# First pair's query parts in another order, and twelve units' transposes copied by ScalarE, in a fused attention and feed-forward kernel

## The reference

```python
c_q = hidden_states @ w_q_down                       # 512 -> 192
q_nope = (c_q @ w_q_up_nope) ...                     # 32 heads of 128
q_rope = _apply_rope(c_q @ w_q_up_rope ...)          # 32 heads of 64, rotary
c_kv = hidden_states @ w_kv_down                     # 512 -> 64
k_rope = _apply_rope(hidden_states @ w_k_rope)
q_lat = einsum('bhsd,hdr->bhsr', q_nope, wuk)
scores = (q_lat . c_kv + q_rope . k_rope) / sqrt(192)
probs = softmax(where(causal, scores, min))
out_lat = einsum('bhst,btr->bhsr', probs, c_kv)
out = einsum('bhsr,hdr->bhsd', out_lat, wuv) @ w_out
```

## Time and profile before

| | |
|---|---|
| median of three timed runs | 1170.35 us |
| the profiled execution's own time | 1167.57 us |
| its span, first to last instruction | 1165.8 us |
| mean granted clock of TensorE | 0.992 of full speed |
| TensorE busy with matmuls | 1105.7 us, 95% |
| VectorE, GpSimd, ScalarE busy | 908.2, 740.0, 623.9 us |
| period from batch to batch | 272.9 us |

### The profile page before, as it was taken

One profiled execution on the slowest core, in us unless ns is written; L12 is line 12 of the kernel. 1 busy time (PEld: TensorE's weight loads), 2 busy tenths in 40 slices (PEclk: granted clock), 3 DMA queues, 4 the chain that ended last, 5 costly groups with the idle time before them and its releaser, 6 DMA issues.

```text
span 1165.8 us, 21866 instructions
## 1 busy us (share of the span) xinstructions
PE 1105.7 (95%) x7284; PEld 906.6 (78%) x7284; DVE 908.2 (78%) x2667; ACT 623.9 (54%) x1733; POOL 740.0 (63%) x951
## 2 busy tenths in 40 slices
PE   5896999999998999999999899999999899999997
PEld 4755788888797788888788678888888678888876
DVE  4767888888676888878776888788867787888855
ACT  3554655555454655555535555655545466555542
POOL 2406977887432978787631887787723598877841
PEclk9998999999999999999999999999999999999998
DMA  9660000000101000000101000000010100000000
GB/s 286 179 194 1 1 1 1 1 1 1 37 10 64 2 1 2 1 1 1 37 1 37 37 2 1 2 1 2 1 37 28 47 1 1 1 1 2 1 1 37
DMA packets 22248, 30.96 MB, mean 27 GB/s; under 512 B 9302, under 2 KB 11094, under 8 KB 21498
## 3 DMA queue, kind: packets, MB, share of 16 engines
q1 hardware_dynamic: 19770, 24.85, 6.7%
q10 hardware_dynamic: 2368, 4.72, 1.2%
HBM read 22.23 MB, written 4.19 MB: 23 GB/s over the span
## 4 chain that ended last, share of the span: by engine, by line
PE 79%; DVE 7%; POOL 7%; ACT 3%; issue 2%; SPq 1%; DMA 1%; POOLq 0%; DVEq 0%
PE Y L983 15%; PE Y L957 12%; PE XZ L942 11%; PE Y L906 10%; PE XZ L922 6%; PE XZ L923 6%; PE XZ L921 5%; PE Y L675 4%; POOL prob L631 3%; PE XZ L675 2%; POOL qT_lo L542 2%; PE XZ L650 2%; POOL q_sums L537 2%; DVE xT_lo L1281 1%; ACT xT_hi L1037 1%
## 5 line engine op out<-in xcount | busy, mean ns | idle before, releaser
L1228 ACT ACTIVATE prob<-XZ,small 128x512 f32<-128x512 f32 (+3 forms) x512 | 266.3, 525 | 282.8 <-DVE small L1622 282.8
L631 POOL TENSOR_TENSOR prob<-prob,small 128x512 f32<-128x512 f32 (+3 forms) x512 | 360.7, 721 | 50.1 <-DVE small L1576 40.4
L1622 DVE CUSTOM_DVE_ANT_0 XZ<-XZ,mask 128x512 f32<-128x512 f32 (+3 forms) x512 | 247.9, 506 | 114.6 <-PE XZ L923 110.5
L537 POOL TENSOR_TENSOR q_sums<-q_sums,q_turned 64x512 f32<-64x512 f32 (+2 forms) x130 | 164.2, 1263 | 201.5 <-DVE q_turned L1564 200.1
L942 PE MATMUL XZ<-ident,prob 128*128 128x128 f32 x1280 | 196.3, 276 | 3.2 <-POOL prob L631 2.9
L921 PE MATMUL XZ<-kT_hi,qT_hi 128*128 128x512 f32 (+3 forms) x512 | 176.9, 345 | 12.7 <-ACT prob L1228 6.8
L542 POOL TENSOR_TENSOR qT_lo<-q_sums,qT_hi 128x512 fp32r<-128x512 f32 (+2 forms) x130 | 165.2, 1271 | 31.9 <-ACT qT_hi L1195 31.8
L942 PEld LDWEIGHTS XZ<-ident,prob 128*128 128x128 f32 x1280 | 149.5, 140 | 43.2 <-POOL prob L631 10.6
L922 PE MATMUL XZ<-kT_lo,qT_hi 128*128 128x512 f32 (+3 forms) x512 | 165.4, 323 | 0.0
L923 PE MATMUL XZ<-kT_hi,qT_lo 128*128 128x512 f32 (+3 forms) x512 | 165.2, 323 | 0.0
L957 PE MATMUL Y<-probT,ckv 128*64 128x384 f32 (+2 forms) x1280 | 152.3, 384 | 0.0
(11 more groups left out here) (220 smaller groups left out, 2162.0 us busy)
## 6 DMA issues: line engine op xcount, KB each, us to landing
wout_nat<-in_L_attn_w_out_dram SPq DMA_DIRECT2D x16, 512.0 KB, 5.0
out_dram<-x_sb SPq DMA_DIRECT2D x16, 256.0 KB, 2.0
x_next<-_attn_hidden_states_dram SPq DMA_DIRECT2D x12, 256.0 KB, 3.4
x_sb<-x_next SPq DMA_DIRECT2D x12, 256.0 KB, 2.3
wbase_nat<-in_L_ffn_W_base_dram ACTq DMA_DIRECT2D x1, 1024.0 KB, 5.7
x_sb<-_attn_hidden_states_dram ACTq DMA_DIRECT2D x4, 256.0 KB, 7.0
nope_a<-_L_attn_w_q_up_nope_dram ACTq DMA_DIRECT2D x1, 1024.0 KB, 5.4
rope_a<-_L_attn_w_q_up_rope_dram SPq DMA_DIRECT2D x1, 1024.0 KB, 8.0
```

Source lines behind the costliest of these rows:

```text
L537: nc.gpsimd.tensor_tensor(q, q, turned, ALU.add).then_inc(q_sum_set, 1)
L631: last = nc.gpsimd.tensor_tensor(prob[u % RING][:, c:c + w], prob[u % RING][:, c:c + w], inv_sum[:, u % RING, m:m + 1].broadcast_to([P, w] ...
L1228: last = nc.scalar.activation(prob[u % RING][:, c:c + w], score_ps[u % 2][:, c:c + w], ACT.Exp, bias=neg_max[:, u % RING, m:m + 1], scale= ...
L1622: last = nc.vector.tensor_tensor_reduce(bank, bank, mask[:, S - w:S], -1.0, HIGHEST, ALU.add, ALU.min, neg_max[:, u % RING, m:m + 1])
```

## The change

Five things change. The opening's parts are taken in the order head 0 early, head 0 late, head 1 late, head 1 early; `ckT_low` of the last tile goes ahead of head 1's early rotary, and the late products write a bank of their own, `XZ[1]`. In batches 1 to 3, head 1 is likewise split into a late and an early part for VectorE, GpSimd and ScalarE (its products stay whole); `update_rows` of the last tile moves into slot 1 of the next attention, behind that unit's maximum and the reciprocal of unit 0. In pair 0, the next pair's first queries are issued in slot 1 and not 0, and GpSimd and ScalarE do their part of the next queries after the scaling and the exponential of the slot. Units 0 to 11 of each batch are all copied by ScalarE. The waits of TensorE follow the parts (`first_parts_done`), and `pv` of pair 0 waits for `x_updated`. The diff, cut to its core:

```diff
-ACT_COPIES = (1, 1, 2, 2, 3)
-DVE_COPIES = (0, 1, 1, 2, 2)
+ACT_FIRST = 12
+BY_ACT = tuple(w < ACT_FIRST or w % UNITS in ACT_BANKS for w in range(UNITS * PAIRS))
...
-        FIRST_PARTS = ((0, EARLY), (1, EARLY), (0, LATE), (1, LATE))
+        FIRST_PARTS = ((0, EARLY), (0, LATE), (1, LATE), (1, EARLY))
+        NEXT_PARTS = ((0, ALL), (1, LATE), (1, EARLY))
...
+        def first_parts_done(b, u):
+            return ({0: 2, 1: 3, 3: 4} if b == 0 else {0: next_part(b, 0) + 1, 1: next_part(b, 1) + 1,
+                                                        3: next_part(b, 2) + 1}).get(u)
...
@@ GpSimd @@
+                def queries_by_parts(m, parts):
+                    for j, (head, cols) in enumerate(parts):
                         if j:
-                            before, where = FIRST_PARTS[j - 1]
-                            qT_low(j - 1, before, 0, where)
-                            pool.wait_ge(qT_lo_set, j)
-                        q_sum(j, head, 0, cols)
-                    qT_low(3, 1, 0, LATE)
+                            pool.wait_ge(qT_lo_set, m + j)
+                        q_sum(m + j, head, 0, cols)
+                        qT_low(m + j, head, 0, cols)
...
+                def query_work(b, g, u, scaled):
+                    k, p = u % UNITS, u // UNITS
+                    m = q_index(b, BODY_PAIRS * g + p + 1, k // 2)
+                    if k % 2:
+                        qT_low(m, k // 2, (p + 1) % 2)
+                    else:
+                        pool.wait_ge(prob_scaled, scaled)
+                        q_sum(m, k // 2, (p + 1) % 2)
...
+                        queries = k < 4 and within(g, u, UNITS * LAST_PAIR - 1)
+                        if queries and known(g, u, UNITS):
+                            query_work(b, g, u, 80 * b + BODY * g + u)
                         if within(g, u, SLOTS - 1):
...
                             last.then_inc(prob_scaled, 1)
+                        if queries and not known(g, u, UNITS):
+                            query_work(b, g, u, 80 * b + BODY * g + u + 1)
...
@@ TensorE, opening @@
-                    for j, (head, cols) in enumerate(FIRST_PARTS):
-                        if j == 2:
-                            transpose_down(-1, STEPS - 1)
-                            pe.wait_ge(ckT_hi, ST)
-                            pe.wait_ge(ckT_lo, ST)
-                        if j >= 2:
-                            pe.wait_ge(q_rot_set, j - 1)
-                        q_products(j, 0, head, qT_ps[head], cols)
+                    for head in range(2):
+                        q_products(0, head, qT_ps[head], EARLY)
+                    transpose_down(-1, STEPS - 1)
+                    pe.wait_ge(ckT_hi, ST)
+                    pe.wait_ge(ckT_lo, ST)
+                    for head in range(2):
+                        q_products(0, head, XZ[1][:, head, :], LATE)
...
@@ TensorE, pv @@
+                    else:
+                        pe.wait_ge(x_updated, 8 * b + 4)
...
@@ TensorE, slots @@
-                        if k in (0, 2) and queries:
-                            m = q_index(b, n, k // 2)
-                            if not known(g, u, 1):
-                                pe.wait_ge(x_updated, 8 * b + 4)
-                            pe.wait_ge(q_rot_set, m - 1)
-                            q_products(m, n, k // 2, qT_ps[k // 2])
+                        if queries and k == (0 if known(g, u, UNITS) else 1):
+                            if not known(g, u, UNITS):
+                                pe.wait_ge(x_updated, 8 * b + 3 if b else ST)
+                            pe.wait_ge(q_rot_set, q_index(b, n, 0) - 1)
+                            q_products(n, 0, qT_ps[0])
+                        if queries and k == 2:
+                            pe.wait_ge(q_rot_set, q_index(b, n, 1) - 1)
+                            q_products(n, 1, qT_ps[1])
...
@@ ScalarE, mixed_steps @@
-                    qT_high(q_index(b + 1, 0, 0), 0, 0)
-                    z_high(b, ORDER[-1])
-                    qT_high(q_index(b + 1, 0, 1), 1, 0)
+                    for j, (head, cols) in enumerate(NEXT_PARTS):
+                        if j == 1:
+                            z_high(b, ORDER[-1])
+                        qT_high(next_part(b + 1, j), head, 0, cols)
...
@@ ScalarE, slots @@
-                        if k in (2, 4) and queries:
+                        rounding = k in (2, 4) and queries
+                        if rounding and known(g, u, UNITS):
                             qT_high(q_index(b, n1, k // 2 - 1), k // 2 - 1, (p + 1) % 2)
...
+                        if rounding and not known(g, u, UNITS):
+                            qT_high(q_index(b, n1, k // 2 - 1), k // 2 - 1, (p + 1) % 2)
                         if copies and k != 2:
                             copy_probT(act, nc.scalar, b, g, v)
...
@@ VectorE, opening @@
-                    for j, (head, cols) in enumerate(FIRST_PARTS):
-                        if j == 2:
-                            ckT_low(-1, STEPS - 1)
-                        q_rotary(j, head, 0, qT_ps[head], cols)
+                    q_rotary(1, 0, 0, qT_ps[0], EARLY)
+                    ckT_low(-1, STEPS - 1)
+                    for head in range(2):
+                        q_rotary(3 + head, head, 0, XZ[1][:, head, :], LATE)
+                    q_rotary(2, 1, 0, qT_ps[1], EARLY)
...
@@ VectorE, mixed_steps @@
-                    q_scaled(q_index(b + 1, 0, 1), 1, 0, XZ[1][:, 1, :])
+                    q_rotary(q_count(b + 1, 0, 1) + 1, 1, 0, XZ[1][:, 1, :], LATE)
+                    update_rows(b, ORDER[-2])
                     z_low(b, ORDER[-1])
-                    q_turns(q_index(b + 1, 0, 1), 1, 0, XZ[1][:, 1, :])
-                    update_rows(b, ORDER[-2])
-                    update_rows(b, ORDER[-1])
+                    q_rotary(q_count(b + 1, 0, 1) + 1, 1, 0, XZ[1][:, 1, :], EARLY)
...
@@ VectorE, slots @@
-                        if k in (0, 2) and queries:
+                        if g == 0 and u == 1 and b:
+                            update_rows(b - 1, ORDER[-1])
+                        if queries and k == (0 if known(g, u, UNITS) else 1):
                             if not known(g, u, UNITS):
-                                dve.wait_ge(x_moved[k // 2], 32 * b + 1)
-                            q_rotary(q_index(b, n1, k // 2), k // 2, (p + 1) % 2, qT_ps[k // 2])
+                                dve.wait_ge(x_moved[0], 32 * b + 1)
+                            q_rotary(q_count(b, n1, 0) + 1, 0, n1 % 2, qT_ps[0])
+                        if queries and k == 2:
+                            if not known(g, u, UNITS):
+                                dve.wait_ge(x_moved[1], 32 * b + 1)
+                            q_rotary(q_count(b, n1, 1) + 1, 1, n1 % 2, qT_ps[1])
```

More of the change, by code:

```diff
@@ L593, in opening @@
                     rough_deviations(2, DOWN, ST)
-                    opening_queries()
+                    queries_by_parts(0, FIRST_PARTS)
                 def mixed_steps(b):
@@ L880, in steps @@
                         if i == MIXED - 1:
[L881 removed]
+                            q_products(0, 1, XZ[1][:, 1, :])
                         products(b, s, 1)
@@ L897, in last_steps, with q_products @@
                     steps(b, LAST_ORDER)
-                def q_products(m, n, head, bank, cols=slice(0, S)):
+                def q_products(n, head, bank, cols=slice(0, S)):
                     hi, lo, rest = (w[:, 2 * n + head, :]
@@ L910, in scores @@
                     n = 80 * b + BODY * g + u
-                    if u % UNITS < 2:
+                    if g == 0 and u < UNITS:
+                        if first_parts_done(b, u):
+                            pe.wait_ge(qT_lo_set, first_parts_done(b, u))
+                    elif u % UNITS < 2:
                         pe.wait_ge(qT_lo_set, q_index(b, BODY_PAIRS * g + u // UNITS, u % UNITS) + 1)
@@ L926, in bank_copies @@
                 def bank_copies(b, g, v):
-                    pair = 16 * b + BODY_PAIRS * g + v // UNITS
-                    return 3 * pair + ACT_COPIES[v % UNITS], 2 * pair + DVE_COPIES[v % UNITS]
+                    done = BY_ACT[:BODY * g + v + 1]
+                    return b * sum(BY_ACT) + sum(done), b * (SLOTS - sum(BY_ACT)) + len(done) - sum(done)
                 def transpose_probs(b, g, v):
@@ L1214, in work @@
                             oT_high(b, g, p)
-                        if k in (2, 4) and queries:
+                        rounding = k in (2, 4) and queries
+                        if rounding and known(g, u, UNITS):
                             qT_high(q_index(b, n1, k // 2 - 1), k // 2 - 1, (p + 1) % 2)
                         v = u - T_LAG
-                        copies = known(g, u, T_LAG) and within(g, u, SLOTS - 1 + T_LAG) and v % UNITS in ACT_BANKS
+                        copies = known(g, u, T_LAG) and within(g, u, SLOTS - 1 + T_LAG) and BY_ACT[BODY * g + v]
                         if copies and k == 2:
```

(12 more changed lines are left out.)

35 lines of the change are left out of this document (11 added, 24 removed).

## The result

The changed kernel takes 1178.74 us (median of four runs, 1177.52 to 1180.31) against 1169.62 us (1168.53 to 1170.57) of the kernel before, run beside it: ratio 1.0079, 95% interval 1.0065 to 1.0092. It is slower, by 9.1 us or 0.8%. The forecast was 1178.4.

What follows compares the result with a forecast made beforehand. TensorE was taken as the bound, with VectorE and GpSimd pacing each batch's first units. Batch 0 at -1.1 us and batches 1 to 3 at +3.07 each made +8.1, so 1178.4 us; own range 1175 to 1181.5.

Steps and rivals of the forecast that it cites:

- The three costs: Pair 0 to pair 1: late update +1.32 us in batches 1 to 3; GpSimd's order +0.75, ScalarE's copies +1.0 in all four.
- the side: Whole kernel: slower by more than 2.3 us, the side of the forecast and the first rival, chance 0.72.
- Opening of batch 0: Start of batch 0's attention: unit 0 starts near 94.0, 2.77 us earlier; head 1's rotary 2.86 earlier, taken as the term.
- I keep the half clock for these matmuls: Batch 0's first units: TensorE stays at 1.2 GHz, 0.43 us per matmul; at full clock about 0.6 us more gain.
- the list of what widens the range: Gaps before unit 5 grow to about 3 us in batches 1 to 3; each may bring half clock, 0 to 0.6 each.
- The late update: Batches 1 to 3: VectorE waits for x_moved[1] before head 1's rotary, until 378.65 in batch 1; +1.32 us each, bounds 0 to 2.0.
- GpSimd's order: Pair 0, all batches: scaling goes before head 1's sum, unit 6 1.26 us later; +0.75 at pv of pair 0, bounds 0 to 1.3.
- ScalarE's copies: All batches: copies of units 6 and 8 lie on ScalarE's chain to pv of pair 1; +1.0 us each, bounds 0 to 1.5.
- the new order of head 1's parts brings nothing: Opening of batches 1 to 3: no gain; unit 0's exponential starts at 372.7 against 372.55 before.
- The rival of the other side: Units 1 to 12: VectorE is the limit, freed copies and earlier maxima pay; 3.5 us gained, 1166.9 us, chance 0.18.
- The first two rivals: First: landing or copies hidden, 1174.4 us, chance 0.22. Second: both hidden, opening's gain and order remain, 1170.5 us, chance 0.10.

Runs made afterwards that it cites:

- fifth run: Changed kernel with the last tile's update of x one place earlier in slot 1, ahead of the reciprocal of unit 0's sums: 1174.81 us, ratio 1.0058.
- first: Changed kernel with the last tile's update of x put back at the end of the mixed steps: 1169.42 us, ratio 1.0011.
- ninth run: Changed kernel with update, copies and GpSimd's and ScalarE's order put back, and batch 0 issuing the next pair's queries in slot 0: 1162.66 us, ratio 0.9950.
- third run: Changed kernel with GpSimd's and ScalarE's old order from slot 2 on put back: 1178.23 us, ratio 1.0084.
- second run: Changed kernel with ACT_FIRST = 0, so VectorE copies units 1, 3, 6, 8 and 11 again: 1175.01 us, ratio 1.0056.
- sixth run: Changed kernel with the update of x and the copies put back, GpSimd's and ScalarE's new order kept: 1165.36 us, ratio 0.9980.
- twelfth: Kernel before with the new opening and head 1's split in batches 1 to 3, next queries in slot 0 in every batch: 1160.28 us, ratio 0.9930.
- fourth: Changed kernel with update, copies and GpSimd's and ScalarE's order all put back; opening, split of head 1 and slot 1 stay: 1164.32 us, ratio 0.9964.
- eighth run: Kernel before with only the copies changed, ScalarE copying the first twelve units: 1172.34 us, ratio 1.0035.
- seventh to twelfth: Seventh: kernel before with only the opening's order changed, 1166.92 us; tenth: kernel before with only slot 1 in batches 1 to 3, 1178.00; eleventh: both edits, 1175.29.

## Why the prediction was right, and where it was not

**Total and side.** 1178.4 forecast, 1178.74 measured. The three costs stand in the traces with the causes given, and the side is right for these reasons. That the total is within 0.4 us is luck. The forecast added 8.1 us to 1170.35; the measured difference is 9.1, from 1169.62. In the profiled executions batch 0 gained nothing in place of 1.1, and batches 1 to 3 lost 2.96, 3.38 and 3.97 in place of 3.07 each, 10.3 in all for 8.1. Behind that are a late update that cost more than its term and a gain that the prediction didn't have.

**Opening of batch 0.** Forecast 2.86 earlier through unit 0 at 94.0; it came at 93.91, and the opening alone gives 3.02. Right. But batch 0 as a whole was to gain 1.1, and at pv of pair 1 it gained nothing (40.01 against 40.04). Two steps of the prediction failed here. The first is a sum behind "I keep the half clock for these matmuls". It takes 0.43 us for each product of unit 1, but ends the five products of head 0, which start at 96.72, at 98.3; at 0.43 each they end at 98.9. Head 1's rotary, put at 101.58, came at 102.18, which is the 0.6 missing. The second is the clock behind unit 5: the 0.50 came again at 107, behind the wait of 1.67 us, and from head 1's rotary to pv of pair 0 the change lost 1.21 in place of 0.75. The fifth run, with 3.4 us at the half clock in batch 0 and not 10.2, has the forecast 1.1 (38.96). In the list of what widens the range the clock stood for batches 1 to 3 only.

**The late update.** Place, cause and wait were right: second update near 373.7 (373.22), DMA wait of 1.32 (1.32), rotary near 378.6 (378.21). The term was mis-sized. Putting the update back gives 1.89 to 3.65 us, for three reasons. The update also stands on VectorE's list ahead of head 0's rotary, 0.6 us. TensorE's longer wait for unit 5, 3.1 us, is followed by the half clock, 3.4 us of it in batch 1 and 6.8 in batch 2, and batch 2 loses 0.6 more with the same wait. And in batch 3 the wait is 2.85: there the store before it took 3.50 us to land, not 1.98. The Trainium skill (DMA: Bandwidth & Descriptors, section on the anatomy of one DMA) puts most of a fixed cost of 2.0 us down to the receipt of the write, for transfers that GpSimd issues. By the estimate of 2.6 us for each transfer that its figures give, the wait would have been 2.2. The measured 1.32 and 1.33 in batches 1 and 2 go by the rows of before (2.0 and 2.3); the store of 3.50 in batch 3 agrees with neither.

**GpSimd's order.** Forecast 1.26 at unit 6 and 0.75 at pv of pair 0. With the landing in time and the full clock, unit 6 starts 8.26 us behind head 1's rotary and not 6.90, so 1.36 later (first and ninth run, batch 1), and pv of pair 0 is 0.98 later. The mechanism was right and the term a little small. It costs nothing while the update is late (third run), and there the prediction added a term that another covers: TensorE's own work behind unit 5, at the half clock, lets unit 6 start about as late as the low part did.

**ScalarE's copies.** Forecast 1.0, measured 0.97 from pair 0 to pair 1 (12.55 against 11.58), through the chain given, and 0.84 to 0.88 in the periods of the second run. Right. In batch 0 of the second run it shows only as 0.10, since there pv of pair 0 starts 28.33 us behind the first rotary, against 27.47. The work which VectorE has back doesn't explain it: the sixth run has the same copies on VectorE and 27.21. What differs is the half clock, 13.7 us against 10.2 in both others.

**Missed: a gain in batches 1 to 3.** The prediction said the new order of head 1's parts brings nothing, since unit 0's exponential isn't earlier. It isn't; but head 1's rotary of the next pair, from which all that follows is timed, starts 1.11 us earlier behind the low-rank product in the ninth run, and 1.51 in the twelfth. In slot 1 VectorE fills its wait for head 0's products with unit 1's maximum, which the split has made possible; in slot 0 that wait is gone, since TensorE no longer waits for the last update. The low-rank product itself is 0.2 us later with the new order of parts, so in the period of batch 1 it is 0.85 and 0.95 in the fourth and ninth run. I had looked only at who waits for the exponential and not at the gap between 371.77 and 373.46 on VectorE and what ended it.

For batch 1 the steps from run to run are -0.85 (before to fourth), +0.94 (order), +0.98 (copies) and +1.89 (late update), 2.96 in all. Each is taken from the run before it, so their sum is the measured 275.85 - 272.89 by construction and proves nothing. Taken alone, the copies cost 0.88 in the same batch (eighth run), but taking the order alone out of the changed kernel makes the period 0.36 longer, not shorter: the size of a step depends on which others are there.

**The rival of the other side** (VectorE is the limit) was wrong as put: the freed copies on VectorE bring nothing, the eighth run is slower. The first two rivals fell as well: neither the landing nor the copies were hidden. What was hidden, while the update is late and in batch 0, is the order.

## What to carry to other kernels

Before an instruction is moved later to shorten an engine's list, follow what it signals: here one 0.6 us addition fed a store and a move in series on a DMA queue, and their 4 us turned cover of 1.2 us into a wait. A gain can lie not in the first consumer but in what stands behind it in the in-order queues, so look at each wait near the change, who ends it and by which semaphore: here a product waited for two updates where one was enough. The same goes for issuing work a slot later, which cost 3 us a batch or more when its forerunner was late and 0.3 when it was early. Costs found one at a time don't add while another covers them: put back several together as well as each alone. And for differences of some tenths of a per cent, set the stretches at the half clock side by side before an edit is credited with them.

## What the runs showed of the hardware

- The granted clock differed between two profiled executions of the same list of instructions: 0.50 in one and 1.00 in the other for the 3 us behind a wait of 1.67 us of TensorE that both had. The changed kernel and the runs one to four had 0.50 to 0.56 in the window 107 to 110, the sixth 0.73, the fifth 1.00, and the six in which slot 0 holds the next queries of batch 0 (seventh to twelfth) 1.00 too.
- A stretch at the half clock costs by what TensorE has to do in it. In the ninth run batches 1 and 2, at the full clock, had periods of 271.94 and 271.96, and batch 3, with the same instructions and 3.4 us at 0.50, 272.88. In batch 1 of the sixth run the same 3.4 us fell ahead of a wait for unit 6 and cost nothing: pv of pair 0 came 19.81 us behind the low-rank product, against 19.82 at the full clock in the first run.
- A store of 256 KB that is issued 0.4 us ahead of a move landed after 1.98 us in batch 1 and after 3.50 in batch 3 of one execution; the move took 2.3 and 3.7. In batch 3 a packet of 16 KB of an instruction queue (q8) started at 927.1, while both were under way. The fourteen traces hold 336 such stores and moves between 200 and 1000 us: all 59 that took longer than usual (over 2.05 us for a store, 2.36 for a move) had a packet of an instruction queue (q8 or q14, 8 or 16 KB) under way at the same time, and of the other 277 ten had. No run was made to try it, so the cause isn't shown.
